# Attention heads shared out anew between TensorE and the DMA engines, and one PSUM copy given to VectorE

## The reference

```python
q = (x @ Wq + bq).reshape(1, B * N, H, hd)            # H = 16 heads, hd = 16
kv = (cond @ Wkv + bkv).reshape(1, -1, 2, H, hd)
...
q = _fq_sym(q, axis=-1); k = _fq_sym(k, axis=-1); v = _fq_sym(v, axis=2)
attn = jnp.einsum('bhqd,bhkd->bhqk', q, k)            # 1024 queries x 1024 keys for each head
attn = jax.nn.softmax(attn.astype(jnp.float32), axis=-1)
attn = _fq_unsigned(attn, axis=-1)                    # rounded to 0..255
out = jnp.einsum('bhqk,bhkd->bhqd', attn, v)
out = jnp.transpose(out, (0, 2, 1, 3)).reshape(B, N, C)
return out @ Wp + bp
```

## Time and profile before

| | us |
|---|---|
| median of 3 runs | 434.83 |
| lowest and highest | 431.51, 436.91 |
| the profiled execution, its own time | 439.01 |
| its span, first to last instruction | 437.2 |

### The profile page before, as it was taken

One profiled execution on the slowest core, in us unless ns is written; L12 is line 12 of the kernel. 1 busy time (PEld: TensorE's weight loads), 2 busy tenths in 40 slices (PEclk: granted clock), 3 DMA queues, 4 the chain that ended last, 5 costly groups with the idle time before them and its releaser, 6 DMA issues.

```text
span 437.2 us, 7553 instructions
## 1 busy us (share of the span) xinstructions
PE 314.7 (72%) x2629; PEld 191.9 (44%) x2629; DVE 351.8 (80%) x567; ACT 321.3 (73%) x516; POOL 123.1 (28%) x295
## 2 busy tenths in 40 slices
PE   4979986786274885747867776876768675785956
PEld 2655554521163874533434444453434443532433
DVE  4567999289999675754869989998998899869992
ACT  3585689754143364596979998999999999978861
POOL 6242444100010121000123656221312222328320
PEclk9998999597667998995689989699988999999576
DMA  8700022000020001112799999899989995900011
GB/s 279 306 2 2 1 96 97 0 1 0 0 97 0 1 2 18 31 25 48 195 201 160 158 151 169 139 159 143 175 137 147 150 170 106 168 18 1 24 37 36
DMA packets 115638, 39.92 MB, mean 91 GB/s; under 512 B 110480, under 2 KB 114192, under 8 KB 114832
## 3 DMA queue, kind: packets, MB, share of 16 engines
q1 hardware_dynamic: 115168, 38.85, 45.1%
q0 software_dynamic: 144, 0.52, 0.3%
q10 hardware_dynamic: 288, 0.07, 0.1%
HBM read 11.11 MB, written 1.05 MB: 28 GB/s over the span
## 4 chain that ended last, share of the span: by engine, by line
DVE 30%; ACT 23%; PE 23%; issue 17%; POOL 3%; DMA 3%; SPq 0%; ACTq 0%; DVEq 0%; POOLq 0%
ACT rb L886 15%; DVE nm L1346 4%; PE ps L1852 3%; PE ps L1828 2%; DMA stage<-rb 2%; DVE rb L1271 2%; DVE rb L1258 2%; DVE rb L1269 2%; PE ps L1864 2%; PE ps L1748 2%; DVE gs L1249 2%; PE ps L1932 2%; DVE ra L1431 1%; DVE small L1433 1%; DVE st L1003 1%
## 5 line engine op out<-in xcount | busy, mean ns | idle before, releaser
L1346 DVE TENSOR_REDUCE nm<-ps 128x1 f32<-128x1024 f32 x128 | 153.3, 1217 | 15.4 <-PE ps L1852 14.9
L886 ACT ACTIVATE rb<-ps,eb,sq 128x1024 int16<-128x1024 f32 x128 | 153.7, 1213 | 13.3 <-POOL eb L565 12.5
L1852 PE MATMUL ps<-ra,rb 128*128 128x512 bf16 x256 | 86.8, 426 | 41.4 <-ACT rb L886 40.8
L565 POOL TENSOR_SCALAR eb<-nm,sq 128x1 f32<-128x1 f32 x128 | 34.1, 267 | 134.1 <-DVE nm L1346 132.8
L1852 PEld LDWEIGHTS ps<-ra,rb 128*128 128x128 bf16 x256 | 16.1, 101 | 59.7 <-ACT rb L886 57.5
L1877 PEld LDWEIGHTS ps<-ra,tern 128*128 128x128 f16 x624 | 26.4, 99 | 16.2 <-issue 5.0
L1748 PE MATMUL ps<-xqT,tern 128*128 128x512 bf16 x64 | 21.0, 475 | 8.9 <-DVE rb L1258 7.6
L886 ACT ACTIVATION_READ_ACCUMULATOR rb<-ps,eb,sq 128x1 f32 x128 | 26.9, 210 | 0.0
L1877 PE MATMUL ps<-ra,tern 128*128 128x16 f16 x624 | 26.5, 171 | 0.3 <-DMA tern<-rb 0.3
L1864 PEld LDWEIGHTS ps<-idh,rb 128*128 128x128 f16 x256 | 17.8, 105 | 16.6 <-issue 10.5
L1864 PE MATMUL ps<-idh,rb 128*128 128x128 f16 x256 | 21.7, 233 | 4.7 <-issue 2.5
(11 more groups left out here) (224 smaller groups left out, 716.2 us busy)
## 6 DMA issues: line engine op xcount, KB each, us to landing
stage<-w SPq DMA_DIRECT2D x2, 1024.0 KB, 4.8
rb<-ra SPq DMA_DIRECT2D x16, 128.0 KB, 2.9
rb<-wide_rows SPq DMA_DIRECT2D x1, 1536.0 KB, 8.3
xs<-x SPq DMA_DIRECT2D x4, 256.0 KB, 4.0
cx<-ctx_in SPq DMA_DIRECT2D x4, 256.0 KB, 4.4
stage<-w_gate SPq DMA_DIRECT2D x1, 1024.0 KB, 7.3
stage<-w_up SPq DMA_DIRECT2D x1, 1024.0 KB, 10.2
stage<-w_down SPq DMA_DIRECT2D x1, 1024.0 KB, 4.7
```

The source lines that it names most:

```text
L565: nc.gpsimd.tensor_scalar(eb[:, u % 3:u % 3 + 1], nm[:, u % 3:u % 3 + 1], sq[:, t, h:h + 1], LN255, ALU.mult, ALU.add).then_inc(s_bias, 1)
L886: A(esc[u % E_RING], bank(2 * (u % 3), 2), ACT.Exp, bias=eb[:, u % 3:u % 3 + 1], scale=sq[:, t, h:h + 1], accum_out=es[:, t % 2, h:h + 1]) ...
L1346: V.tensor_reduce(nm[:, u % 3:u % 3 + 1], bank(2 * (u % 3), 2), AX.X, ALU.max, negate=True).then_inc(s_max, 1)
L1852: ins = M(bank(2 * (u % 3) + hf), qz[t % 2][:, h // 2, h % 2, :], kT[:, h // 2, 512 * hf:512 * hf + 512], start=True, stop=True)
```

## The change

Heads 1, 3, 5, 12 and 15 of each tile are turned over TensorE, where it was 1, 4, 12 and 15, and the other 11, not 12, by DMA. The copy of head 3 out of bank 7 is made by VectorE, behind the row maxima of head 6; ScalarE still makes four copies per tile, that of head 5 behind the exponential of head 7, where that of head 4 stood behind the exponential of head 6.

```diff
-ON_TENSOR = (1, 4, 12, 15)
+ON_TENSOR = (1, 3, 5, 12, 15)
+COPIED_BY_VECTOR = 3
...
+def copied_by_vector(w):
+
+    return by_tensor(w) and (w % H == COPIED_BY_VECTOR or w == U - 1)
...
                 w = u - MOVE_LAG
-                if 0 <= w < U - 1 and by_tensor(w):
+                if 0 <= w < U and by_tensor(w) and not copied_by_vector(w):
                     move(w)
...
+            def move(w):
+                dve.wait_ge(s_tr, turned_by_tensor(w))
+                if w >= R_RING:
+                    dve.wait_ge(s_av, w - R_RING + 1)
+                V.tensor_copy(rT[w % R_RING].bitcast(I32), bank(7).bitcast(I32)).then_inc(s_moved, 1)
+
             def attention(u):
...
                     V.tensor_reduce(nm[:, u % 3:u % 3 + 1], bank(2 * (u % 3), 2), AX.X, ALU.max,
                                     negate=True).then_inc(s_max, 1)
+                if TR_LAG <= u < U and copied_by_vector(u - TR_LAG):
+                    move(u - TR_LAG)
...
-            def last_move():
-                dve.wait_ge(s_tr, turned_by_tensor(U - 1))
-                dve.wait_ge(s_av, U - R_RING)
-                V.tensor_copy(rT[(U - 1) % R_RING].bitcast(I32), bank(7).bitcast(I32)).then_inc(s_moved, 1)
-
...
-            last_move()
+            move(U - 1)
```

## The result

| | before | changed |
|---|---|---|
| median of 4 runs, us | 435.87 | 444.97 |
| lowest and highest | 431.51, 438.02 | 441.82, 452.67 |
| profiled execution, span | 437.2 | 440.0 |

The ratio is 1.0183, with a 95% interval of 1.0114 to 1.0252: slower by 1.1 to 2.5%, where +0.7% was forecast and 442.2 us was the upper end.

A forecast was written before the change was run, and what follows sets the result against it. No single engine: a ring of three heads, with ScalarE nearly always busy and VectorE close behind. Terms 0 + 1.0 + 2.4 - 0.4 = +3.0 us, added to the 434.83 median, gave 437.8 us, range 433.3 to 442.2.

The forecast's parts named there:

- The DMA: One transposing DMA fewer per tile would change nothing, 0 us, being hidden seven heads deep.
- The copy on VectorE: Between maxima of heads 6 and 7, taking 0.61 us: +0.16 per ordinary tile, +0.76 per layernorm tile.
- the late copy of head 5: ScalarE's copy now follows head 7's exponential; in an ordinary tile head 8's exponential starts at 302.36, against 302.20.
- the wait of TensorE: At place 9, transposes wait for head 5's copy; including this, +0.25 per ordinary tile and +0.8 per layernorm tile.
- The wait before head 7: Sign in layernorm tiles' profile: head 7's exponential waits 0.6 to 0.9 us for GpSimd.
- the pauses before L1894: Sign in the profile: TensorE idle about 0.7 us or more before `o_transposes`, put down to ScalarE's copy.
- The clock of TensorE: New transposes in TensorE's idle stretches may prevent a fall to half clock: -0.4 us, bounds -1.2 to +2.4.
- slow rival: TensorE's wait before `o_transposes` lets its clock fall in most tiles: 7 tiles by 1.0 to 1.5, 444 to 449; chance 0.11.

The follow-up runs named there:

- e5: Changed kernel plus eight useless 128x256 matmuls on TensorE per tile, before the finished tile's two transposes: 440.58 us against 437.76 before, ratio 1.0083.
- e3: Changed kernel with the three layernorm tiles' heads as before, only the other five tiles changed: 437.81 us against 438.57 before, ratio 0.9990.
- e4: Changed heads and VectorE copy only in the three layernorm tiles, the other five as in the kernel before: 443.82 us against 437.76, ratio 1.0179.
- e0: Changed kernel run again without edit: 444.85 us against 438.57 before, ratio 1.0162.
- e6: Kernel before plus eight useless 128x128 matmuls behind the scores of head 6 in every tile: 436.28 us against 437.76, ratio 0.9962.
- e7: Changed kernel with layernorm tiles' heads as before and the finished tile's two transposes one place later in all tiles: 437.78 us against 437.76, ratio 0.9986.
- e9: Kernel before, but ordinary tiles use heads 1, 3, 12, 15 over TensorE with VectorE copying head 3: 436.48 us against 439.91, ratio 0.9970.
- e10: Kernel before plus useless matmuls at head 6, at heads 4 and 5 of layernorm tiles, and at the second tile's start: 435.16 us against 439.91, ratio 0.9925.
- e11: Kernel before with e9's heads in ordinary tiles and the useless matmuls of e10: 437.50 us against 439.91, ratio 1.0061.
- e8: Changed kernel with head 5 by DMA again, VectorE's copy of head 3 kept in every tile: 442.91 us against 439.91 before, ratio 1.0145.
- e2: Changed kernel with the finished tile's two transposes one place later in TensorE's order: 440.02 us against 438.57 before, ratio 1.0138.

## Why the prediction was wrong

**The DMA: right.** The transposing DMAs land 3.0 us at least and 3.3 in the median after their issue, as before, and no gain from one fewer is seen.

**The copy on VectorE, the late copy of head 5 and the wait of TensorE: right in size.** 0.60 us where 0.61 was taken. The stretch from head 4 to 8 of a tile with layernorm grew by 0.81, forecast 0.8. An ordinary tile at full clock takes 21.53 instead of 21.33, +0.20, forecast 0.25. The wait before head 7 is 0.77, the pauses before L1894 0.88 and 1.30 us. These terms make 3 x 0.9 + 4 x 0.2 = 3.5 us, where the sum had 3.4. The median of e5 is +2.8 as a whole.

**The clock of TensorE: this term failed, in sign and size.** The sum had -0.4 for it. Measured, it cost 2.5 to 3.2 us. In the two profiled executions the stretches from head 8 to 14 sum to 26.8 us after and 24.0 before, where 22.8 (e5) and 22.4 (e3) are the sums without a fall: 4.0 us of falls against 1.5, so +2.5 in one pair of executions. In the medians e4 is 3.2 us above e5. In the profiled executions of the changed arrangement 9 of 9 such tiles fell in this stretch (the changed kernel, e0, e4); with the arrangement of before 5 of 21 (before, e3, e6, e7, e9, e10, e11, some with filler), where five more had the half clock only earlier in the tile, where it cost nothing.

I had read the new transposes as filling TensorE's idle stretch and so keeping the clock. In tile 2, from which the -0.4 was taken, the fall was gone in the changed kernel's profile, but the tile took 21.87 against 22.00, so 0.1 and not 0.4 came of it; and e3, with the same transposes in tile 2, fell there and took 23.13. The prediction also counted three falls in the loop before. There were more: the clock was at half up to 215.9 us and again from 222.7, in the first two tiles.

In a tile with layernorm the transposes did not make up for the copy: from head 4 to 8 TensorE is idle 6.81 - 3.86 = 2.95 us in spite of eight transposes more, where it was 6.00 - 3.23 = 2.77, and the pause before L1894 comes on top. But the difference is small, and other profiles with tiles as before show up to 2.99 (e3, e9) without a fall behind it. That this is why the clock falls is argued and not shown. Shown are three things: filling the pause took the falls away (e5, one profile), the pause isn't needed (e8), and the late head 7 isn't enough each time (e2). The prediction named such a mechanism in its slow rival, priced it per tile about right (1.0 to 1.5; measured 0.8 to 2.2), but gave it 0.11, and thought it would need all seven tiles to matter. Three were enough. That the median, 444.97, lies in that rival's 444 to 449 is partly luck, since tiles 2, 4 and 6 did not fall and the base was low.

The rule that the prediction quotes from the Trainium skill, "TensorE: Matmul & The Clock Gate", Part 4: PE-mode transpose, would have set the term to 0 and the sum to +3.4. That was nearer than mine, by a little. No run here shows whether the rule holds: filler made of matmuls at head 6 did not save tile 3 either (e6, e10).

**The base.** The sum was added to a median of 3 (434.83). Over 86 executions in three sessions the kernel before has medians of 438.57, 437.76 and 439.91, so some of the distance from forecast to result is in the base; the difference of medians within one session, +6.3 (e0, six executions against 29) and not +9.1, is the better size of the effect. Added to 434.83 it would give 441.1, inside the range: the failed term and the low base together took the result out of it.

What stays open: what in the copy on VectorE makes the clock fall so much more often between heads 8 and 14, why a tile with layernorm of the kernel before falls in some executions and not in others, and how the loss divides in executions that had no profile. The division above is from profiled ones.

## What to carry to other kernels

Before work is moved to an engine, look for the tiles where that engine is already the one that all wait for: most tiles had room for the copy, three of eight had none, and those three carried the loss as far as the medians can tell (e3, e4). When an edit makes one engine late, price also what the others do while they wait: here TensorE's clock fell in those tiles as well, which cost about as much again as the delay itself (2.5 to 3.2 us against 2.7). Where executions of one kernel scatter by 2 to 3%, take the base from many of them before adding a sum of 3 us to it, and compare profiles over the stretch that was changed.

## What the runs showed of the hardware

- Work of no use on TensorE made a kernel faster: eight matmuls of 128x256 per tile in a pause of 1.3 us took a loss of about 6 us to 2.8 (e5, medians). Filler at head 6, at heads 4 and 5 of three tiles and in front of a wait for a DMA gave a ratio of 0.9925 to the kernel before (e10), but 1.0061 with other heads in the ordinary tiles (e11).
- The granted clock went from 1.00 to 0.5, which is 2.4 to 1.2 GHz, within a busy loop in which TensorE was never idle for more than 1.5 us at a time in the heads of that tile before the fall (tiles 3, 5 and 7 of the changed kernel). At the lower level two matmuls of 128x512 took 1.04 instead of 0.60, and eight transposes of 128x128 1.06 instead of 0.61.
- The same half clock cost nothing in one part of a tile and 0.8 to 2.2 us in another. From head 4 to 8 of tile 3, with VectorE busy throughout, the stretch took 5.85 at 0.52 (before) and 5.85 at 1.00 (e10); from head 8 to 14 it took 7.45 at full clock and 8.31 to 9.72 with a fall.
- Between executions the stretch behind the loop, the same in all these kernels but for the order of a few instructions, took 54.2 to 62.0 us; in the longest (e5, 62.0) the clock stood at half from 381 to 398 us.
- A copy of 128x512 int32 from PSUM took VectorE 0.67 to 0.69 us listed and ScalarE 0.58 to 0.59; the next instruction started 0.60 and 0.47 us after it.
